# Queries and keys by way of a scratch tensor in HBM, another order of the query chunks, and a plan that prefers maxima

## The reference, cut to what matters

```python
def _L1_attn_ref(x, Wq, Wk, Wv, Wo):        # x: layernorm of the residual, (1, 2048, 256)
    q = _rope(proj(Wq)); k = _rope(proj(Wk)); v = proj(Wv)
    scores = jnp.einsum('bhsd,bhtd->bhst', q, k) * attn_scale
    scores = jnp.where(causal, -jnp.inf, scores)
    probs = jax.nn.softmax(scores, axis=-1)
    out = jnp.einsum('bhst,bhtd->bhsd', probs, v)
    return out.transpose(0, 2, 1, 3).reshape(B, S, E) @ Wo.T
```

## Time and profile before

| what | us |
|---|---|
| median of 3 runs (lowest, highest) | 2329.78 (2329.5, 2344.99) |
| the profiled execution | 2334.38 |
| its span | 2332.6 |
| PE busy in the span | 1940.5 (83%) |
| VectorE, ScalarE, GpSimd busy | 1613.1, 909.5, 1005.9 |
| attention projections begin, in the span | 1582.4 |
| attention heads begin | 1760.8 |
| attention output begins | about 2276 |

### The profile page before, as it was taken

The page is one execution under the profiler, slowest core; times in us unless marked ns, Lnnn a source line. Parts: engine busy times, 40 slices in busy tenths (PEclk is TensorE's granted clock), DMA queues, the critical chain, the costliest instruction groups (busy, mean ns, idle before and its releaser), DMA issues. The chain is left out here.

```text
span 2332.6 us, 33316 instructions
## 1 busy us (share of the span) xinstructions
PE 1940.5 (83%) x10072; PEld 1106.1 (47%) x10072; DVE 1613.1 (69%) x2774; ACT 909.5 (39%) x1866; POOL 1005.9 (43%) x908
## 2 busy tenths in 40 slices
PE   4748998999999999999999999567314889999996
PEld 3634555555555555555555554455202433444435
DVE  6667878777778778687787785775103687778735
ACT  1223443443444433434434334111001346677771
POOL 0023685795775857956857766012101201001110
PEclk8868999999999999999999999678655678799998
DMA  2100000000000000000000000111221000000001
GB/s 84 65 8 5 8 1 5 9 1 5 8 1 12 1 5 8 1 5 8 1 5 0 1 1 1 39 39 32 49 46 37 22 8 12 12 8 15 15 2 37
DMA packets 33624, 36.14 MB, mean 15 GB/s; under 512 B 10816, under 2 KB 25664, under 8 KB 33344
## 3 DMA queue, kind: packets, MB, share of 16 engines
q1 hardware_dynamic: 32272, 33.14, 5.3%
q10 hardware_dynamic: 1200, 1.31, 0.2%
HBM read 19.21 MB, written 2.10 MB: 9 GB/s over the span
## 5 line engine op out<-in xcount | busy, mean ns | idle before, releaser
L1177 POOL TENSOR_TENSOR lath_summed<-lath_summed,lath_probs 128x512 f32<-128x512 f32 (+3 forms) x528 | 584.3, 1128 | 119.0 <-ACT lath_probs L1100 108.9
L1100 ACT ACTIVATE lath_probs<-lath_shifted 128x512 f32<-128x512 f32 (+3 forms) x640 | 357.6, 565 | 682.8 <-DVE lath_shifted L1211 641.9
L1211 DVE TENSOR_TENSOR lath_shifted<-lath_score,lath_shift 128x512 f32<-128x512 f32 (+3 forms) x640 | 385.2, 607 | 145.5 <-PE lath_score L986 130.1
L1218 DVE TENSOR_REDUCE lath_maxima<-lath_max 128x1 f32<-128x512 f32 (+3 forms) x640 | 380.2, 605 | 130.0 <-PE lath_max L1007 82.9
L1822 ACT ACTIVATE atth_probs<-atth_score 128x512 f32<-128x512 f32 (+3 forms) x640 | 293.7, 540 | 204.6 <-PE atth_score L1742 202.4
L1783 DVE TENSOR_REDUCE atth_maxima<-atth_slot 128x2 f32<-128x1024 f32 (+3 forms) x288 | 287.2, 1043 | 87.9 <-PE atth_slot L1725 86.9
L994 PE MATMUL lath_out<-lath_probs,lat_latent 128*64 128x512 f32 (+3 forms) x1280 | 306.5, 558 | 0.0
L1007 PE MATMUL lath_max<-lat_key_hi,lath_query_hi 128*128 128x512 f32 (+3 forms) x640 | 265.4, 423 | 17.9 <-DVE lath_maxima L1218 16.6
L982 PE MATMUL lath_score<-lath_query_hi,lat_key_hi 128*128 128x512 f32 (+3 forms) x640 | 266.3, 416 | 3.7 <-DVE lath_shifted L1211 3.7
L986 PE MATMUL lath_score<-lath_query_hi,lat_key_lo 128*128 128x512 f32 (+3 forms) x640 | 256.2, 400 | 0.0
L983 PE MATMUL lath_score<-lath_query_lo,lat_key_hi 128*128 128x512 f32 (+3 forms) x640 | 237.4, 371 | 0.0
(11 more groups left out here) (332 smaller groups left out, 2579.3 us busy)
## 6 DMA issues: line engine op xcount, KB each, us to landing
att_key<-attp_k_hi SPq DMA_DIRECT2D x128, 32.0 KB, 2.0
atth_query<-atth_q_hi SPq DMA_DIRECT2D x128, 32.0 KB, 2.0
ffn_a_w<-in_L_ffn_W SPq DMA_DIRECT2D x2, 1024.0 KB, 11.3
lat_raw_out<-in_L_attn_w_out SPq DMA_DIRECT2D x8, 256.0 KB, 2.6
lat_rope<-in_c_rope_feature SPq DMA_DIRECT2D x1, 2048.0 KB, 9.9
ffn_b_w<-in_L_ffn_W SPq DMA_DIRECT2D x2, 1024.0 KB, 7.1
mix_a_factors<-in_L_ffn_factors SPq DMA_DIRECT2D x8, 256.0 KB, 4.4
att_key<-attp_k_lo SPq DMA_DIRECT2D x64, 32.0 KB, 2.0
```

The costliest lines, as they stand in the source:

```text
L1100: nc.scalar.activation(probs[:, prob_slot(j, kt), h, q0:CH], shifted[:, 2 * (kt % 2) + h, q0:CH], ACT.Exp, scale=SCALE0).then_inc(s["exp_d ...
L1177: last = nc.gpsimd.tensor_tensor(summed[:, j % 2, h, q0:CH], so_far, probs[:, prob_slot(j, kt), h, q0:CH], ALU.add)
L1211: nc.vector.tensor_tensor(shifted[:, 2 * (kt % 2) + h, q0:CH], score_bank[score_place(j, kt, h) % 3][:, q0:CH], shift[:, j % 2, h, q0:CH], ...
L1218: nc.vector.reduce_max(maxima[:, h, i, kc:kc + 1], max_bank[(i * (nj + 1) + kc) % 2][:, 0:width], AX.X).then_inc(s["maxima_taken"], 1)
```

## The change

- The scratch tensor `att_scratch` in HBM holds all queries and keys, 512 rows by 2048 tokens, once rounded and once as the rest. For each chunk ScalarE rounds all four banks into `high`, VectorE writes the rests of all four into `low`, and SyncE writes each to the scratch tensor with one DMA (1 MB each). When both have landed, six DMAs of 256 KB read the chunk's keys from there into `key`: for each part of the three and each half of the 128 partitions, 16 rows by 8 pairs of heads by 512 tokens.
- In the heads, queries come from the scratch tensor too, a whole chunk of 16 heads at a time, into one of two query tiles: six DMAs a chunk. GpSimd no longer splits. A unit's shift goes in four DMAs instead of eight. The first two chunks are issued at the start, the third after the shift of unit 4, the fourth after that of unit 8, each once the scores of the chunk two before are done.
- The units run by query chunk 1, 3, 2, 0 instead of 0, 3, 2, 1.
- The planner prefers maxima (-0.2) to scores (-0.1) and scores to values (0.0); before it was scores (-0.05), maxima (0.0), values (0.1). It may look ahead by up to two chunks of queries.

```diff
-UNITS = [(c, g) for c in (0, 3, 2, 1) for g in range(NG)]
-QUERY_TILES = 4
+UNITS = [(c, g) for c in (1, 3, 2, 0) for g in range(NG)]
-PREFER = {"turn": -0.3, "finish": -0.3, "scores": -0.05, "maxima": 0.0, "values": 0.1}
+PREFER = {"turn": -0.3, "finish": -0.3, "scores": -0.1, "maxima": -0.2, "values": 0.0}
-    query_ready = {n: 8.0 + 2.5 * n for n in range(QUERY_TILES)}
+    query_ready = {n: 6.0 if n < NG else 9.0 for n in range(2 * NG)}
-                if kt == key_tiles(j) - 1 and n + QUERY_TILES < units:
-                    query_ready[n + QUERY_TILES] = end + 5.0
+                if kt == key_tiles(j) - 1 and n % NG == NG - 1 and n + NG + 1 < units:
+                    query_ready.update({m: end + 8.0 for m in range(n + NG + 1, n + 2 * NG + 1)})
...
+def place_parts(sp, to, scratch, base, half, part, kept, to_columns, columns):
+    of = scratch[kept, base:base + DIM, columns].rearrange("(r a c) t -> a c r t", a=2, c=D1)[half]
+    return sp.dma_start(to[head_rows(half, D1 * part, D1), :, to_columns].bitcast(F32), of)
...
# projections, SyncE, for each chunk
-                    sp.wait_ge(s["k_high_done"], 2 * c + 2)
-                    sp.wait_ge(s["k_low_done"], 2 * c + 2)
-                    for h in range(H1):
-                        half, rows = h // 8, slice(D1 * (h % 8), D1 * (h % 8) + D1)
-                        for part, of in enumerate((k_hi, k_lo, k_hi)):
-                            sp.dma_start(key[head_rows(h, D1 * part, D1), h // 2, cols].bitcast(F32), of[rows, half, :].bitcast(F32)).then_inc(s["keys_placed"], 16)
+                    for sem, of, part, kept in (("high_done", high, 0, "high_kept"), ("low_done", low, 1, "low_kept")):
+                        sp.wait_ge(s[sem], 4 * (c + 1))
+                        sp.dma_start(scratch[part, :, cols].rearrange("(f p) t -> p f t", p=P), of[:].bitcast(F32)).then_inc(s[kept], 16)
+                    sp.wait_ge(s["high_kept"], 16 * (c + 1))
+                    sp.wait_ge(s["low_kept"], 16 * (c + 1))
+                    for half in range(2):
+                        for part in KEY_PARTS:
+                            place_parts(sp, key, scratch, DIM, half, part, KEY_PARTS[part], cols, cols).then_inc(s["keys_placed"], 16)
# projections, VectorE
-                        for half in range(2):
-                            dve.wait_ge(s["k_high_done"], 2 * c + half + 1)
-                            nc.vector.tensor_tensor(k_lo[:, half, :], bank[2 + half][:], k_hi[:, half, :].bitcast(F32), ALU.subtract)\
-                              .then_inc(s["k_low_done"], 1)
+                        if c >= 1:
+                            dve.wait_ge(s["low_kept"], 16 * c)
+                        for f in range(4):
+                            dve.wait_ge(s["high_done"], 4 * c + f + 1)
+                            nc.vector.tensor_tensor(low[:, f, :], bank[f][:], high[:, f, :].bitcast(F32), ALU.subtract).then_inc(s["low_done"], 1)
# projections, ScalarE
-                        for half in range(2):
-                            if c >= 1:
-                                act.wait_ge(s["keys_placed"], 16 * 3 * H1 * c)
-                            nc.scalar.activation(k_hi[:, half, :], bank[2 + half][:], ACT.Copy).then_inc(s["k_high_done"], 1)
-                        for half in range(2):
-                            nc.scalar.activation(q_t[:, half, c * CH:(c + 1) * CH], bank[half][:], ACT.Copy).then_inc(s["q_taken"], 1)
+                        if c >= 1:
+                            act.wait_ge(s["high_kept"], 16 * c)
+                        for f in range(4):
+                            nc.scalar.activation(high[:, f, :], bank[f][:], ACT.Copy).then_inc(s["high_done"], 1)
...
# heads, SyncE
+                def place_queries(m):
+                    c = UNITS[NG * m][0]
+                    if m >= 2:
+                        sp.wait_ge(s["scores_done"], GROUP * (last_step[NG * (m - 1) - 1] + 1))
+                    for half in range(2):
+                        for part in QUERY_PARTS:
+                            place_parts(sp, query[m % 2], scratch, 0, half, part, QUERY_PARTS[part], slice(0, CH), slice(c * CH, (c + 1) * CH))\
+                              .then_inc(queries_placed[m % 2], 16)
+
+                place_queries(0)
+                place_queries(1)
...
-                        if n >= 1 and n - 1 + QUERY_TILES < len(UNITS):
-                            place_queries(n - 1 + QUERY_TILES)
+                        if n % NG == 0 and 1 <= n // NG < NCH - 1:
+                            place_queries(n // NG + 1)
```

More of the change, by code:

```diff
@@ L1437, in attention_stage @@
         attended = sb("attended", [P, NT, DIM])
-        attention_projections(core, q_t, key, v_one, w_o_t, attended)
-        attention_heads(core, q_t, key, v_one, attended)
+        attention_projections(core, scratch, key, v_one, w_o_t, attended)
+        attention_heads(core, scratch, key, v_one, attended)
         attention_output(core, attended, w_o_t)
@@ L1586, in attention_projections, with attention_heads @@
     core.end_step()
-def attention_heads(core, q_t, key, v_one, attended):
+def attention_heads(core, scratch, key, v_one, attended):
     nc = core.nc
@@ L1609, in sb @@
             return core.sb(f"atth_{name}", shape, dt, ctx)
-        query = sb("query", [P, QUERY_TILES, 2, CH], F32R)
-        q_hi, q_lo = sb("q_hi", [P, 2, CH], F32R), sb("q_lo", [P, 2, CH], F32R)
-        maxima = sb("maxima", [P, 2, GROUP, TPC, NCH + 1])
-        row_max = sb("row_max", [P, 2, GROUP, TPC])
-        shift = sb("shift", [P, 2, GROUP, 2, TPC])
+        query = [sb(f"query{i}", [P, H1 // 2, CH], F32R) for i in range(2)]
+        maxima = sb("maxima", [P, 2, 2, 2, TPC, NCH + 1])
+        row_max = sb("row_max", [P, 2, 2, 2 * TPC])
+        shift = sb("shift", [P, 2, 2, 2, 2 * TPC])
         shift_t = sb("shift_t", [2 * GROUP * TPC, 2, P], F32R)
@@ L1633, in query_rows @@
         def query_rows(n, h, count, first, width):
-            return query[head_rows(h, 0, count), n % QUERY_TILES, h // 2, first:first + width]
+            g = UNITS[n][1]
+            return query[n // NG % 2][head_rows(h, 0, count), (GROUP * g + h) // 2, first:first + width]
         def by_head(tensor, c, g):
@@ L1662, in _ @@
                       .then_inc(s["masked"], 1)
-                    if kt == key_tiles(j) - 1 and n % 2 == 1 and n + 5 < len(UNITS):
-                        split((n + 5) // 2)
             @block.sync
             def _(sp):
-                def place_queries(n):
-                    m, g = n // 2, UNITS[n][1]
-                    if n >= QUERY_TILES:
-                        sp.wait_ge(s["scores_done"], GROUP * (last_step[n - QUERY_TILES] + 1))
-                    if n >= 2:
-                        sp.wait_ge(queries_placed[n % 2], per_unit * (n // 2))
-                    for part, of in enumerate((q_hi, q_hi, q_lo)):
-                        sp.wait_ge(s["q_high_done" if part < 2 else "q_low_done"], m + 1)
-                        for h in range(GROUP):
-                            first = D1 * (GROUP * (g % 2) + h)
-                            sp.dma_start(query[head_rows(h, D1 * part, D1), n % QUERY_TILES, h // 2, :].bitcast(F32),
-                                         of[first:first + D1, m % 2, :].bitcast(F32))\
-                              .then_inc(queries_placed[n % 2], 16)
-                for n in range(QUERY_TILES):
-                    place_queries(n)
+                def place_queries(m):
[8 more added lines that the diff above has]
+                place_queries(1)
                 for e in plan["vector"]:
@@ L1731, in _ @@
                         pe.wait_ge(s["shift_ready"], n + 1)
-                        nc.tensor.transpose(slot[r % 2][0:2 * GROUP * TPC, 0, 0:P], shift[:, n % 2].rearrange("p h c i -> p (h c i)"), core.ident)\
+                        nc.tensor.transpose(slot[r % 2][0:2 * GROUP * TPC, 0, 0:P], shift[:, n % 2].rearrange("p a c i -> p (a c i)"), core.ident)\
                           .then_inc(s["filled"], 1)
@@ L1782, in _ @@
                                 at = 2 + kc if what == "whole" else 1
-                                nc.vector.reduce_max(maxima[:, n % 2, heads, i, at], slot[r % 2][:, :, begin:begin + width], AX.X)\
+                                nc.vector.reduce_max(maxima[:, n % 2, :, pair, i, at], slot[r % 2][:, :, begin:begin + width], AX.X)\
                                   .then_inc(s["slot_taken"], 1)
```

62 lines of the change are left out of this document (27 added, 35 removed).

## The result

The changed kernel takes **2273.47 us** (median of 4 runs, 2270.61 to 2285.01); the kernel before, beside it, 2331.45 (2329.5 to 2344.99). The ratio is 0.9748, 95% interval 0.9698 to 0.9799: faster by 58 us. The forecast was 133 us faster; the time lies above the range. The profiled span is 2270.8 us against some 2200 forecast, so 70 us are to be explained.

A forecast was written before the change was run, and what follows sets the result against it. SyncE issuing DMAs bounds the projections; PE bounds the heads where the clock is full, before that their start. 2334.4 - 76 (projections) - 56 (heads) = 2202, with the median 4.6 lower: 2198 us; range 2172 to 2248.

The forecast's parts named there:

- Issue count: Projections: 32 DMA issues replace 192 key DMAs, 5 us per chunk; the bound moves back to PE and the evacuation.
- a term that I had only in the lower end: Projections: PE staying at the low clock, a tile's four wide matmuls taking 3.62 us instead of 1.88; lower end 45 saved.
- The last write and its read: Projections' end: last write landed at 1676.4, its read at 1684.2, heads starting at 1685 instead of 1761, 76 us saved.
- B: Projections: HBM traffic at half rate, 113 GB/s, 32.5 us per chunk, nothing saved there, 2274 us; chance 0.07.
- C: Key reads: 16 target partitions put each read on one DMA engine, 24 GB/s, heads 166 us later, 2440; chance 0.03.
- First queries: Heads' start: six DMAs bring the first query chunk in 7.8 us; first scores 32 us after the start, against 38.
- The 24 to 25 us between the first maxima and the first scores: Heads' start: 24 wide and the diagonal maxima matmuls come ahead of the first score, taking 24 us.
- Middle: Heads up to the last maxima: 332 us of PE work, plus 12 for VectorE's slots, 9 and 5 for the clock.
- the 14 that I had allowed (9 and 5): Heads' middle, low clock: 9 us before the clock rises (5 to 13), 5 after shift waits (0 to 22).
- one of my signs of being wrong: Heads: the forecast is wrong if the clock keeps falling at unit boundaries.
- Rival A: Heads' middle: VectorE becomes the bound, reaching only its present 0.81, 39 us more, 2237 us; chance 0.20.
- End: Heads' tail: 145 scores left after the last maxima instead of 68, taking 69 us against 41.

The follow-up runs named there:

- e9: Changed kernel with each read's 16 rows placed in every third partition instead of 16 in a row: 2254.8 us, ratio 0.9668.
- e4: Changed kernel with a chunk's key reads as eight 256 KB DMAs into all 128 partitions, keys misplaced and exponential scale 0: 2257.22 us in one run.
- e5: Changed kernel with half of the scratch reads, those of the upper 64 partitions, on ScalarE's queue: 2269.43 us, ratio 0.9697.
- e11: Changed kernel with old chunk order and preferences, reads into every third partition, and the upper half's reads on ScalarE's queue: 2239.74 us, ratio 0.959.

## Why the prediction was wrong

By its own steps; times are moved by the 4.4 us of the later beginning where they are compared.

1. **Issue count: right.** Waits of ScalarE for key DMAs are gone, 32 issues do for 192, and the second and third evacuation come 17.5 us after the one before (forecast 16). The 1.6 us more are a term that I had only in the lower end: behind the evacuation, after 3.57 us idle, TensorE runs at the low level, and the first tile's four wide matmuls take 3.53 us instead of 1.88.
2. **The last write and its read: the step that failed.** I took 384 GB/s for both directions from the earlier trace rows, whose loads fill 128 partitions, and 4.6 us for the landing of the last read, from a row of one lone 256 KB load. For six in a row, each into 16 partitions, the rate counts: 119 GB/s, 13.2 us for a chunk, and with the writes (2.1 MB at some 385 GB/s, 5.4 us) a chunk keeps the DMA engines busy for 18.7 us, longer than the 17.5 between evacuations, and than the 13.4 between the last two. It shows three times. The last evacuation starts at 1677.2, 5.1 us late. ScalarE waits 5.0 us for the scratch write there, but TensorE's last transposes end only at 1674.6, so 2.5 are due to the write; the other 2.6 are the longer periods of step 1. In e9 the same evacuation waits for TensorE alone. That chunk's writes are done 22.5 us after the evacuation's start instead of 8.8, and the read takes 16.1 instead of 8.3. Together some **26.5 us, 24 of them from the rate: heads at 1711.4 instead of 1685.** I had put the bandwidth question only as rivals B and C. C named what mattered, the 16 target partitions, but priced it at 24 GB/s, a fifth of the measured 119, and I dismissed it by the earlier trace rows (a 16-row DMA lands in 2.0 us). Those DMAs are of 32 KB, an eighth of the reads, and go out one every 0.63 us, 52 GB/s: they never asked for the rate.

   The Trainium skill has this very case, and I did not weigh it: "SBUF — State Buffer", section "Door 1: The DMA port swizzle", gives a transfer to partitions 0 to 15 four of sixteen ports, 104 GB/s measured and 109 at most. Here it was 113 to 129, a little above that, and e4 and e9 agree with the rule in direction (290 to 320 for 128 partitions, 130 to 165 for 16 that are spread). As an estimate by the page, 1.57 MB at 109 GB/s take 14.4 us. The same page's section "Can I just issue two DMAs to hit both halves?" says that a second one adds only 6%. Here two queues gave 182 to 209 GB/s in e5's second query chunk and up to 263 in e11, so the measurement differs.
3. **First queries: the same cause.** 17.8 us instead of 7.8; the first scores 42.4 behind the start instead of 32: **10.4 us.** The 24 to 25 us between the first maxima and the first scores were right.
4. **Middle: right in sum, in part by luck.** 359.5 us against 358, with PE busy 350.7 of it. But the mean clock was 0.93, so the low level cost 25 us, not the 14 that I had allowed (9 and 5): it was there till 1779 and came back in the middle, at 1854 to 1866 and around 2000, one of my signs of being wrong. Less work at full clock (326 against 330) and less idle time (9 against 14) made up for it. Rival A did not come: VectorE reached 315 of 359.5, 0.88, above the 0.81 of A, though below the 0.90 that I had named. The waits for shift DMAs are gone.
5. **End: the second step that failed.** 96 us against 69, **27 us.** There is also a slip in the sum: the 25 full scores that I left to the first unit are 17, since the first score of a diagonal step is 512 wide too and is in its price already. The 145 are then 49 of full steps and 24 diagonal steps of four each; my own prices give 65, so 31 are to be explained. At 0.34 us per us the 50 us at the low level are 17 (against e9's 84.5 us at 0.92 it is 11.5, but e9 has 14 us at the low level itself). Another 8 are the full steps, 12 of them at 2.61 us where I took 1.93, a spacing of the earlier trace rows that holds only while earlier exponentials are in store. Some 4 are the diagonal steps: in e9 at the full level a unit of chunk 0 takes 7.5 us where I took 6.9. The last 2 are not placed.
6. The later beginning, 4.4, and the middle, 1.5. All together 26.4 + 10.4 + 27 + 4.4 + 1.5 = 69.7 of the 70 us.

The case closest to the outcome was B by its time (2274), but it said that the projections save nothing and the heads all; measured, the projections saved 50 and the heads 17. Its closeness is luck.

## What to carry to other kernels

Price a DMA by the partitions that it fills: take the rate from a row with the same target shape, and where there is none, let the range reach down to what was measured here for 16 partitions in a row, 119 GB/s against some 390. Check whether the traffic of a period fits in the period before counting landings, because a queue that is full delays the next write too. Before taking a step's price from one spacing, add up what each engine needs for the step: here ScalarE's 2.06 us already forbade 1.93 as a lasting rate. And where TensorE is over 95% busy, look at the time at the low clock in both profiles before giving a difference of 10 or 20 us to an edit of the order.

## What the runs showed of the hardware

- DMAs of 256 KB from HBM, issued in a row, ran at 113 to 129 GB/s into 16 neighbouring partitions each, at 130 to 165 into 16 spread ones, at 290 to 320 into 128, with the DMA engines shown as 90% busy or more; a row pitch of 9472 bytes in HBM instead of 8192 made no difference.
- Reads on two queues into different halves of SBUF added up to between 104 and 263 GB/s.
- The same instructions took 459.6 and 480.3 us, with 64 and 125 us at the low level of TensorE's clock; over the runs of one kernel the price was 0.27 to 0.34 us per us.
